# Row sums, query sums and put-off ropes in another order on VectorE, sines ahead of weight halves on GpSimd

## What is computed

```python
def reference(x, ctx, mask, g_xattn, g_ffn, wq, wk, wv, wo, route_w, A, Bw):
    # attention: 32 query heads, 8 key/value heads, width 128
    q = rope(heads(layernorm(x) @ wq)); k = rope(heads(ctx @ wk)); v = heads(ctx @ wv)
    attn = softmax(q @ k.T / sqrt(128) + mask)
    x = x + tanh(g_xattn) * ((attn @ v) @ wo)
    # routed low-rank block: top 1 of 8 experts, rank 16
    h = layernorm(x); logits = h @ route_w.T
    weight = one_hot(argmax(logits)) * max(logits)
    x = x + tanh(g_ffn) * sum_e weight[e] * ((h @ A[e].T) @ Bw[e].T)
    return x
# rope(x) = x * cos + rotate_half(x) * sin
```

## Time and profile before

| what | value |
|---|---|
| median of the runs | 1120.96 us (1119.96 to 1121.04) |
| the profiled execution, its own time | 1119.15 us |
| its span in the profile | 1117.2 us |
| TensorE matmul busy | 1093.4 us, 98% |
| VectorE busy | 888.6 us, 80% |
| ScalarE busy | 639.6 us, 57% |
| GpSimd busy | 613.3 us, 55% |
| granted TensorE clock | 9 (the top digit) in all 40 slices |

### The profile page before, as it was taken

How to read it: one execution, slowest core, us unless ns; L and a number is a source line. 1 busy time by engine, 2 the same in 40 slices (tenths; PEclk the granted TensorE clock), 3 DMA queues, 4 the chain that set the end, 5 groups by cost and what they waited for, 6 DMA issues and landing times.

```text
span 1117.2 us, 16963 instructions
## 1 busy us (share of the span) xinstructions
PE 1093.4 (98%) x5616; PEld 915.4 (82%) x5616; DVE 888.6 (80%) x1407; ACT 639.6 (57%) x1112; POOL 613.3 (55%) x519
## 2 busy tenths in 40 slices
PE   7999999899999999999999999999999999999998
PEld 6888888778888888888888787888888888888786
DVE  6876757777778787888888999787777787778886
ACT  6563466666666666666655545555555555555443
POOL 4552388867777777777754433334434434443423
PEclk9999999999999999999999999999999999999999
DMA  7859973685555464646379645453546353533201
GB/s 247 256 218 346 370 251 143 232 310 166 192 167 201 158 205 154 207 152 207 132 258 382 199 141 184 136 193 122 192 118 190 113 185 106 180 113 105 76 1 76
DMA packets 105797, 206.26 MB, mean 185 GB/s; under 512 B 8816, under 2 KB 58096, under 8 KB 99824
## 3 DMA queue, kind: packets, MB, share of 16 engines
q1 hardware_dynamic: 105712, 205.18, 54.6%
HBM read 122.31 MB, written 82.84 MB: 184 GB/s over the span
## 4 chain that ended last, share of the span: by engine, by line
PE 69%; DVE 12%; POOL 7%; issue 6%; ACT 3%; SPq 1%; DMA 1%; DVEq 0%; ACTq 0%; POOLq 0%
PE attn L897 22%; PE proj L831 19%; PE score L848 7%; PE attn L793 5%; PE score L793 3%; PE turned L793 3%; POOL rot L1701 2%; PE attn L882 2%; PE turned L859 2%; PE attn L884 2%; POOL wq_s L1676 2%; DVE row_sum L1172 1%; DVE o_s L1192 1%; DVE q_r L1143 1%; DVE wo_s L1094 1%
## 5 line engine op out<-in xcount | busy, mean ns | idle before, releaser
L897 PE MATMUL attn<-wo_s,o_s 128*128 128x512 f32 x1524 | 375.1, 395 | 0.7 <-DVE o_s L1192 0.7
L831 PE MATMUL proj<-xB,wq_s 128*128 128x512 f32 x1344 | 335.5, 393 | 2.0 <-ACT copies L1483 2.0
L897 PEld LDWEIGHTS attn<-wo_s,o_s 128*128 128x128 f32 x1524 | 281.2, 188 | 57.9 <-DVE o_s L1192 1.1
L831 PEld LDWEIGHTS proj<-xB,wq_s 128*128 128x128 f32 x1344 | 252.7, 188 | 55.9 <-ACT copies L1483 2.7
L1701 POOL TENSOR_TENSOR rot<-rot,tab 128x512 f32<-128x512 f32 x110 | 164.0, 1491 | 172.7 <-ACT rot L1462 172.6
L848 PEld LDWEIGHTS score<-k_r,q_r 128*128 128x128 f32 x1024 | 122.8, 191 | 13.1 <-DVE q_r L1104 7.6
L1461 ACT ACTIVATE rot<-q_r 64x512 f32<-64x512 f32 x85 | 53.6, 630 | 135.1 <-DVE q_r L1143 133.6
L848 PE MATMUL score<-k_r,q_r 128*128 128x64 f32 x1024 | 122.1, 272 | 3.0 <-DVE q_r L1104 3.0
L1184 DVE TENSOR_TENSOR p_low<-turned,p_high 64x512 fp32r<-64x512 f32 x128 | 88.0, 688 | 38.5 <-ACT p_high L1499 36.5
L1507 ACT ACTIVATE o_s<-attn 128x512 fp32r<-128x512 f32 x127 | 69.4, 595 | 80.2 <-PE attn L884 80.2
L1104 DVE TENSOR_TENSOR q_r<-q_r,rot 128x512 f32<-128x512 f32 x85 | 88.3, 1039 | 17.1 <-POOL rot L1701 12.0
(11 more groups left out here) (243 smaller groups left out, 1692.7 us busy)
## 6 DMA issues: line engine op xcount, KB each, us to landing
wq_kept<-wq_s SPq DMA_DIRECT2D x16, 1792.0 KB, 6.2
wq_s<-wq_kept SPq DMA_DIRECT2D x16, 1792.0 KB, 8.5
v_kept<-vst SPq DMA_DIRECT2D x64, 256.0 KB, 4.6
v_s<-v_kept SPq DMA_DIRECT2D x128, 128.0 KB, 4.8
wo_kept<-wo_s SPq DMA_DIRECT2D x32, 512.0 KB, 3.7
wo_s<-wo_kept SPq DMA_DIRECT2D x32, 512.0 KB, 5.4
k_kept<-kst SPq DMA_DIRECT2D x32, 256.0 KB, 2.5
wq_raw<-in_wq SPq DMA_DIRECT2D x16, 512.0 KB, 6.9
```

The lines of the kernel that those rows point to most:

```text
L831: last = e.matmul(dst[:, :], wq_s[:, b % 2, A, s, kt, :], xB[:, B, mv, kt, :], start=(first and kt == 0 and m == 0), stop=(kt == 1 and m = ...
L897: last = e.matmul(out_bank(k, bp)[:, :], o_s[:, s, bp, h, :], wo_s[n % WO_SLOTS][:, m, :], start=(h == 0 and i == 0), stop=(h == GROUP - 1 ...
```

## The change

On VectorE, in the step loop: the low half of `wo` goes behind the row sums in remainder 1 steps; the query sums, the late one of the previous step and the early ones of this step, come right behind the row sums; the put-off rope comes behind all query sums. On GpSimd, in odd steps with weights to split: the sine of (b,1) comes ahead of the weight half that stood between `normalise` and it. No instruction is added or removed.

```diff
-            def rest_of(k):
+            def ropes_left(k):
                 for q in ropes_of(k)[1] + ropes_of(k)[2]:
                     q_cos(*q)
                     q_add(*q)
-                for q in sums_of(k)[1]:
-                    q_sum(*q)
...
                 if k:
-                    for n in wo_late(k - 1):
-                        raw_low(("wo", n))
+                    if k % 4 != 1:
+                        for n in wo_late(k - 1):
+                            raw_low(("wo", n))
                     sum_rows(k)
-                    rest_of(k - 1)
+                    if k % 4 == 1:
+                        for n in wo_late(k - 1):
+                            raw_low(("wo", n))
+
+                    for q in sums_of(k - 1)[1]:
+                        q_sum(*q)
                 for q in early:
                     q_sum(*q)
+                if k:
+                    ropes_left(k - 1)
...
                     normalise(k)
                     if k % 2 == 0 and pieces:
                         combine_weights(pieces[0][0], (1,))
-                    elif pieces:
-                        weight_low(*pieces[0 if k % 4 == 1 else 1])
                     for q in ropes[0]:
                         by_sin(ROPE_NO["q", *q])
+                    if k % 2 and pieces:
+                        weight_low(*pieces[0 if k % 4 == 1 else 1])
```

## The result

The changed kernel takes **1110.11 us** (median of four runs, 1109.50 to 1110.42). The kernel before, run beside it, takes 1120.46 us (four runs, 1119.39 to 1121.04). The ratio is 0.9910, with a 95% interval of 0.9898 to 0.9922: faster by 10.4 us, between 8.7 and 11.4. The sign and the mechanism were as forecast; the size was not, most of all beside the routed block.

A forecast was written before the change was run, and what follows sets the result against it. TensorE's matmuls fill 98% of the span, so only its waits can be won: 3.4 + 3.0 + 0.3 + 0.4 + 0.4 = 7.5 us off 1119.15 gives 1111.6, or 1113.5 us as a median; range 1112.0 to 1118.0.

The forecast's parts named there:

- Part 1: Remainder 1 steps: with row sums ahead of the `wo` half, TensorE's wait for `normalise` goes, 7 × 0.49 = 3.4 us.
- Part 2: Remainder 3: sums first, sine before weight half, no score waits, 3.0 us; step 27 0.3; remainder 0 0.4 us.
- its worse case: Step 23: weight half holds (b,1)'s add, ending near 538.4 us at the latest, otherwise 537.4; scores ready at 538.27.
- Part 3: Steps beside the routed block: VectorE's shorter queue cuts TensorE's waits for `weighted`, between 0 and 1.5 us, taken as 0.4.
- Part 4: The rest: the second half's 24 steps stand at the floor, nothing to win; later `wo` store and weight half cost nothing.
- the likeliest case: The forecast itself, all parts paying: 1113.5 us, its own range 1112.0 to 1115.0, chance 0.67.
- the slower rival: VectorE's queue slips past attention times values; TensorE loses 0.28 us in 30 odd steps, time 1126.0 us; chance 0.07.

The follow-up runs named there:

- no_wo: The full change without the move of the `wo` half (sums and sine moves only); median 1112.75 us, ratio 0.9936 to the kernel before.
- wo_only: The kernel before with only the `wo` half moved behind the row sums in remainder 1 steps; median 1123.80 us, ratio 1.0036.
- sums_only: The kernel before with only the query sums moved ahead of the put-off rope, in every step; median 1121.61 us, ratio 1.0004.
- pool_only: The kernel before with only GpSimd's sine moved ahead of its weight half in odd steps; median 1127.19 us, ratio 1.0062.
- wo_short: The kernel before with the `wo` half behind the row sums and GpSimd's odd-step weight halves cut from 512 to 64 columns; median 1118.11 us, ratio 0.9988.
- step29_old: The changed kernel with VectorE's old order (`wo` half and put-off rope first) in step 29 alone; median 1112.78 us, ratio 0.9937 to the kernel before.
- full_again: The changed kernel itself, unedited, run again; median 1109.35 us, ratio 0.9908 to the kernel before.
- The tail edits: The changed kernel with the tail's last rope add moved up, 1110.28 us; put-off rope too, 1109.84; both plus step 0's weight halves waiting for the rope add, 1110.54.

## Why the prediction was right and where it was wrong

**Part 1 held.** The forecast put the moved `wo` half 5.99 us after the scores, at a price of 0.69 us; it started 6.01 us after them and took 0.64 us. `normalise` was held (1.38 us against the 1.05 it takes beside the sums), as the forecast allowed, and ended 7.55 us after the scores, ahead of the 8.19. Remainder 1 fell by 0.49 us, as computed. The 3.4 us are its share only in the order in which the forecast added the parts: with the sums moved, the `wo` half in its old place loses 0.15 us a step, not 0.49 (no_wo). The sums had won the rest.

**Part 2 held, with a more favourable course.** Remainder 3 fell by 0.60 us, step 27 by 0.27 (forecast 0.3), remainder 0 by 0.10 (forecast 0.07). The sine of step 23 came 2.7 us earlier against the scores, not 2.0, since the row sums were earlier too. The weight half held the add that the scores need (1.60 us), which the forecast had as its worse case, and there was room for it: the add ended 12.09 us after the scores, and they need it at 12.74. `add_out` came 2.1 us earlier, not 0.6 to 1.1.

**Part 3 is the step that failed**, in the size of its term. It said between 0 and 1.5 us, "I take 0.4 us", "since VectorE is the bound there and its work stays the same". It was 2.53 us. Two things were wrong. The upper bound came from one row, `weighted`, 1.5 us. The rows for L1074, 0.5 and 0.2 us, stood beside it, and they are what step 29's shorter queue took away. And the reason for taking the low value was false: where VectorE is the bound, the time for which its instructions are held is on the path, so the hold that the forecast removed in part 2 (1.35 to 0.69 us) had to be counted again in steps 31 and 33. The same 0.7 us, twice, and 1.0 us carried in from step 29, is 2.5 us. With 2.5 in place of 0.4 the forecast would have been 1111.4 us, already below the low end of its own range, 1112.0.

**Part 4** was nearly right: the second half gave 0.2 us, not 0. The floor that the forecast took from the earlier trace rows had a small loss in it: the remainder 0 steps of the second half took 14.15 or 14.16 us and now take 14.12.

**The conversion to the median** was the rest. The executions' own times differ by 8.73 us against the forecast 7.5; the medians by 10.35. The forecast added 1.9 us (1111.6 to 1113.5), since the profiled execution of before stood that far under the median of three runs (1.3 us under that of four); the profiled execution of the changed kernel stands 0.3 us above its own. So the 3.4 us between 1113.5 and 1110.11 are 2.4 us of stages that gave more (2.1 of them part 3) and 2.2 us of this conversion, less the 1.2 us of scatter in the stage table. The forecast's range had its low end at the low end of the likeliest case, with nothing left for that or for part 3.

**The rivals.** The mechanism of the slower rival, VectorE's put-off rope held by GpSimd until TensorE's attention products wait, did not happen in the whole change, but it is what two of the parts do alone: in every remainder 2 step TensorE idles 0.5 us (wo_only) and 0.7 us (sums_only) ahead of these products, and the step is 1.1 to 1.2 us longer. In pool_only it idles 0.4 us there, behind a hold of the present tile's add. The forecast summed its parts as if each could be had alone; that they came out right together was partly luck of which parts were in the change.

## What to carry to other kernels

Where VectorE and GpSimd work from SBUF side by side, cost an order of instructions by who stands beside whom, not by its sum of durations: put those that one engine does not hold (here sums with an input in PSUM, 1.27 us for two) beside the other's work, and those that it holds (0.69 alone, up to 1.82 us) into its gaps. Test such moves together, since each of these three alone was no gain or a loss of 4 to 7 us, and all together were a gain of 10. When bounding a stage, add up all of TensorE's waits in it, and for the first step of a stage ask how late the step before leaves the queue.

## What the runs showed of the hardware

**A held instruction waits for the other engine's instruction.** What sets the add in step 21 of wo_only and wo_short apart (1.59 and 0.69 us) is the length of GpSimd's weight half (1.73 and 0.77 us). It works the other way as well: `normalise` takes 1.04 or 1.05 us beside the query sums and 1.38 us beside the `wo` half or the cosines. An instruction of 8 columns was held for 0.38 us (step 31, L1237, 0.61 us against 0.23). The Trainium skill (SBUF — State Buffer, "Who interferes with whom") says that such instructions exclude each other; the runs agree, and show that by this the kernel's time moves by 1.5% between orders of the same instructions (pool_only against the full change).

**The clock behind a short wait.** In the tail TensorE waits 2.1 us for the rope add, and what it is granted behind that differs between executions of the same kernel. Windows of step 62, for PE alone (length, busy, granted clock, DMA share, GB/s). The changed kernel:

```profile
1051.63:1062.71 11.08, 10.27 (x56) 1.00 0.01 2
```

The same kernel run again:

```profile
1049.42:1061.38 11.96, 11.58 (x57) 0.86 0.01 2
```

And step29_old, which has the same program in the tail:

```profile
1051.82:1065.39 13.57, 13.19 (x57) 0.75 0.01 2
```

In the slower two the matmuls that take 0.39 or 0.40 us at 2.4 GHz take 0.63 us, that is at the level of 1.2 GHz, for part of the step. All 14 traces with this tail fall on these three: 11.08 to 11.10 us at 1.00 (four), 11.95 to 12.04 at 0.86 (four), 13.56 to 13.58 at 0.75 (six). So 0 to 2.5 us come and go there whatever the edit. Step 1 behaves alike behind a wait of 2.7 us: the same instructions took 17.27 us at a granted clock of 0.90 (full_again) and 18.07 us at 0.81 (the changed kernel's first trace). An edit that is worth 1 us needs its steps compared in the trace. The tail edits shortened the wait but did not remove it, and two of their three traces still show the lower clock.
